# A graph attention kernel: attention scores stored word by word instead of turned on TensorE

## The reference

```
h = relu(layernorm(x))
x = x + adj @ norm((adj + adj.T) / 2 + I) @ h       # norm: by the row sums, both sides
h = relu(layernorm(x))
Wh    = h @ W                       # 8 heads of 64 columns
e_src = sum(Wh * a1), e_dst = sum(Wh * a2)          # one score per node and head, each
e     = leaky_relu(e_src[:, None] + e_dst[None, :], 0.2), -9e15 where adj == 0
out_h = elu(softmax(e) @ Wh)
x     = x + dense layers 512-256-128-256-512 (concatenated out_h)
```

## Time and profile before

| | us |
|---|---|
| median of 3 runs | 861.61 (861.1 to 862.35) |
| profiled execution | 862.1 |
| its span, first to last instruction | 860.3 |
| TensorE busy | 839.7 (98%) |
| VectorE busy | 700.0 (81%) |
| ScalarE busy | 428.7 (50%) |
| GpSimd busy | 281.0 (33%) |

### The profile page before, as it was taken

How to read it: one execution, slowest core, us unless ns; L and a number is a source line. 1 busy time by engine, 2 the same in 40 slices (tenths; PEclk the granted TensorE clock), 3 DMA queues, 4 the chain that set the end, 5 groups by cost and what they waited for, 6 DMA issues and landing times.

```text
span 860.3 us, 15286 instructions
## 1 busy us (share of the span) xinstructions
PE 839.7 (98%) x5208; PEld 756.5 (88%) x5208; DVE 700.0 (81%) x1222; ACT 428.7 (50%) x797; POOL 281.0 (33%) x299
## 2 busy tenths in 40 slices
PE   2999999999999999999999999999999999999997
PEld 2888888888888888888899999999999999999786
DVE  6899886557656886586999999999999999998864
ACT  3445433221111112257766666666666666775753
POOL 0000000000000000057875555555556654566422
PEclk9999999999999999999999999999999999999999
DMA  8979931703222222053310000000000032000134
GB/s 344 406 272 375 362 98 50 219 0 122 96 97 92 95 93 89 0 196 126 129 27 25 23 16 26 26 24 25 26 26 25 24 93 68 26 2 6 45 148 149
DMA packets 37675, 87.97 MB, mean 102 GB/s; under 512 B 7216, under 2 KB 8368, under 8 KB 37616
## 3 DMA queue, kind: packets, MB, share of 16 engines
q1 hardware_dynamic: 37616, 87.24, 28.5%
HBM read 74.45 MB, written 12.78 MB: 101 GB/s over the span
## 4 chain that ended last, share of the span: by engine, by line
PE 97%; DMA 1%; DVE 1%; ACT 1%; SPq 0%; issue 0%
PE bank L1877 29%; PE bank L1921 14%; PE bank L77 13%; PE bank L79 13%; PE bank L78 13%; PE bank L554 3%; PE bank L1082 2%; PE bank L1087 2%; PE bank L1083 2%; DMA l_kept<-adj 1%; PE bank L1033 1%; PE bank L2455 1%; PE bank L2449 1%; PE bank L2394 1%; PE bank L2451 1%; PE bank L2420 0%
## 5 line engine op out<-in xcount | busy, mean ns | idle before, releaser
L1397 DVE SCALAR_TENSOR_TENSOR l_q<-bank,e,mask 128x512 fp32r<-128x512 f32 x512 | 339.0, 740 | 22.9 <-PE bank L1877 22.9
L1877 PE MATMUL bank<-l_parts,l_q 128*128 128x260 f32 x2048 | 249.6, 283 | 0.0
L1877 PEld LDWEIGHTS bank<-l_parts,l_q 128*128 128x128 f32 x2048 | 246.7, 188 | 0.4
L77 PE MATMUL bank<-x_hi,s_hi 128*128 128x512 f32 x448 | 174.4, 389 | 0.0
L79 PE MATMUL bank<-x_hi,s_lo 128*128 128x512 f32 x448 | 174.3, 389 | 0.0
L78 PE MATMUL bank<-x_lo,s_hi 128*128 128x512 f32 x448 | 174.3, 389 | 0.0
L805 POOL TENSOR_TENSOR l_prod<-wh,l_a 128x512 f32<-128x512 f32 x29 | 34.0, 1195 | 379.5 <-ACT wh L757 379.5
L1565 ACT ACTIVATE l_o_q<-bank 128x260 f32<-128x260 f32 x128 | 49.0, 388 | 104.0 <-PE bank L1877 96.7
L79 PEld LDWEIGHTS bank<-x_hi,s_lo 128*128 128x128 f32 x448 | 84.1, 188 | 17.6
L78 PEld LDWEIGHTS bank<-x_lo,s_hi 128*128 128x128 f32 x448 | 84.1, 188 | 17.3
L77 PEld LDWEIGHTS bank<-x_hi,s_hi 128*128 128x128 f32 x448 | 84.1, 188 | 17.3
(11 more groups left out here) (234 smaller groups left out, 1179.8 us busy)
## 6 DMA issues: line engine op xcount, KB each, us to landing
rows<-adj_t SPq DMA_DIRECT2D x48, 512.0 KB, 3.8
l_now<-adj SPq DMA_DIRECT2D x16, 512.0 KB, 7.5
l_rows_k<-adj_t SPq DMA_DIRECT2D x16, 512.0 KB, 8.3
l_src<-e_rows SPq DMA_DIRECT2D x32, 256.0 KB, 3.2
l_kept<-adj SPq DMA_DIRECT2D x12, 512.0 KB, 13.2
wh_store<-wh SPq DMA_DIRECT2D x4, 1040.0 KB, 6.2
l_h<-x SPq DMA_DIRECT2D x4, 1024.0 KB, 17.3
x<-x SPq DMA_DIRECT2D x1, 4096.0 KB, 13.7
```

The lines of the kernel that those rows point to most:

```text
L77: pe.matmul(acc, hi, rhs_hi, start=first, stop=False, skip_group_check=True)
L1397: v.scalar_tensor_tensor(out=q[:, i, :], in0=bank[S_BANKS[hh]][:], scalar=e[:, i, H + h:H + h + 1], in1=mask[:, i, cols], op0=ALU.is_le, o ...
L1877: return pe.matmul(bank[Q_BANKS[hh][t]][:, 0:PW], q[:, i, t * P:(t + 1) * P], parts[pair_slot][:, i, hh * PW:(hh + 1) * PW], start=i == 0, ...
```

## The change

The turning of scores by TensorE goes, with the copies behind it. `e_rows` becomes an array of 16 tiles x 16 scores x 128 nodes, and SyncE stores straight out of `e`, where a partition holds one node: each run that is written is one word. The first group's first two columns go first, its other 14 columns by tile after `keep_wh(1)`, the other groups whole. `load_src` reads four runs of 128 scores for one of 512. `wa_hi` and `wa_lo` come to lie side by side, so that one product makes hi x hi and hi x lo (32 columns), and VectorE adds both halves when it takes them. A sixth tile is chosen ahead, at k = 13. Waits of ScalarE, GpSimd and TensorE on the turned scores go. The path for rows that overflow, which does not run here, is adapted alike.

```diff
-        e_t = rows[0:2 * H, 2, :]
...
-        wa_hi = sb("l2_wa_hi", [P, KC, 2 * H], F32R, side="right")
-        wa_lo = sb("l2_wa_lo", [P, KC, 2 * H], F32R, side="right")
+        wa_parts = sb("l2_wa_parts", [P, KC, 4 * H], F32R, side="right")
+        wa_hi, wa_lo = wa_parts[:, :, 0:2 * H], wa_parts[:, :, 2 * H:4 * H]
...
-        EARLY_Q = {11: 0, 12: 1, 14: 2, 15: 3, T: 4}
+        EARLY_Q = {11: 0, 12: 1, 13: 2, 14: 3, 15: 4, T: 5}
...
-            def store_e(q):
-                sp.wait_ge(e_copied, q + 1)
-                sp.dma_start(e_rows[:, q * 512:(q + 1) * 512], turned_e(q, e_late)).then_inc(stored if q >= 2 else first_stored, 16)
-            store_e(0)
-            sp.wait_ge(first_stored, 16)
+            def store_scores(tiles, cols, done):
+                count = cols.stop - cols.start
+                if count == 1:
+                    src, dst = e[:, tiles, cols.start], e_rows[tiles, cols.start, :].rearrange("t p -> p t")
+                else:
+                    src = e[:, tiles, cols].rearrange("p t c -> p (t c)")
+                    dst = e_rows[tiles, cols, :].rearrange("t c p -> p (t c)")
+                sp.dma_start(dst, src, allow_slow_non_contiguous=True).then_inc(done, 16)
+            sp.wait_ge(e_ready, 2 * SLOTS + 4)
+            for h in range(2):
+                store_scores(GROUPS[0], slice(h, h + 1), first_stored)
+            sp.wait_ge(first_stored, 32)
             spread_scores(0)
             keep_wh(0)
             keep_wh(1)
+            for t in range(SLOTS):
+                store_scores(slice(t, t + 1), slice(2, 2 * H), stored)
             keep_wh(2)
-            store_e(1)
-            sp.wait_ge(first_stored, 32)
+            sp.wait_ge(e_ready, 2 * 2 * SLOTS + 4)
+            store_scores(GROUPS[1], slice(0, 2 * H), first_stored)
+            sp.wait_ge(first_stored, 48)
             spread_scores(1)
             keep_wh(3)
-            store_e(2)
-            store_e(3)
-            sp.wait_ge(stored, 32)
+            for q in range(2, 4):
+                sp.wait_ge(e_ready, 2 * SLOTS * (q + 1) + 4)
+                store_scores(GROUPS[q], slice(0, 2 * H), stored)
+            sp.wait_ge(stored, 16 * (SLOTS + 2))
...
-                    v.tensor_copy(e[:, t, :], bank[7][:, 0:2 * H]).then_inc(e_ready, 2)
+                    v.tensor_reduce(e[:, t, :], bank[7][:, 0:4 * H].rearrange("p (k c) -> p c k", k=2), AX_X, ALU.add
+                                    ).then_inc(e_ready, 2)
...
-                if k in (8, 13):
-                    take_e_t((k - 8) // 5)
...
-                    mm = split_product(pe, bank[7][:, 0:2 * H], g_hi[:, b, cols], g_lo[:, b, cols],
-                                       wa_hi[:, k, :], wa_lo[:, k, :], k == 0)
+                    pe.matmul(bank[7][:, 0:4 * H], g_hi[:, b, cols], wa_parts[:, k, :], start=k == 0, stop=k == KC - 1,
+                              skip_group_check=True)
+                for k in range(KC):
+                    cols = slice(k * P, (k + 1) * P)
+                    mm = pe.matmul(bank[7][:, 0:2 * H], g_lo[:, b, cols], wa_hi[:, k, :], start=False, stop=k == KC - 1,
+                                   skip_group_check=True)
...
-                if k == 7:
-                    turn_e(range(0, 4))
-                if k == 11:
-                    turn_e(range(4, 8))
-            turn_e(range(8, 12))
...
-                        row = e_rows[r // 4 * 2 + hh:r // 4 * 2 + hh + 1, r % 4 * QW:(r % 4 + 1) * QW]
-                        sp.dma_start(src[:, hh, :], row.to_broadcast([P, QW])).then_inc(src_loaded[hh], 16)
+                        row = e_rows[r % 4 * GT:(r % 4 + 1) * GT, r // 4 * 2 + hh:r // 4 * 2 + hh + 1, :].rearrange("t o p -> o t p")
+                        sp.dma_start(src[:, hh, :].rearrange("p (t n) -> p t n", t=GT), row.to_broadcast([P, GT, P])).then_inc(src_loaded[hh], 16)
...
-                late_scores(a, 2, e_late[:])
...
-                        late_scores(a, 3, e_late[:])
...
-                        if hp == 0 and r == 0:
-                            a.wait_ge(stored, 32)
...
-                p.wait_ge(first_stored, 32)
...
-                        pe.wait_ge(e_copied, 4)
...
-                    q_phase(r, pair_slot, 0, lambda i: last_turns(pe) if isinstance(r, int) and r == 0 and i == G8 else None)
+                    q_phase(r, pair_slot, 0)
```

More of the change, by code:

```diff
@@ L653, in spread_and_project @@
         e_ready = sem("l2_e_ready")
-        e_turned = sem("l2_e_turned")
-        e_copied = sem("l2_e_copied")
         top_ready = sem("l2_top_ready")
@@ L673, in per_head, with sync @@
             return ap.rearrange("p (h d) -> p h d", h=H)
-        def turned_e(q, e_late=None):
-            return (e_t if q < 2 else e_late)[:, q % 2 * 512:(q % 2 + 1) * 512]
-        def sync(sp, spread_scores, keep_wh, e_late):
+        def sync(sp, spread_scores, keep_wh):
             first_sync(sp)
@@ L793, in late_factors @@
             a.activation(fac["D"][:], args[1][:], ACT.Exp, scale=-1.0).then_inc(fac_ready, 1)
[L794 to L797, removed]
         def gpsimd(p, between):
@@ L931, in vector @@
                     v.tensor_tensor(w_lo[:], w_rows, w_hi[:].bitcast(F32), ALU.subtract).then_inc(w_ready, 1)
-                    v.tensor_copy(wa_hi[:], wa[:]).then_inc(w_chain, 1)
+                    v.tensor_copy(wa_hi, wa[:]).then_inc(w_chain, 1)
                 if r == 1:
                     v.wait_ge(w_chain, 4 * KC + 2)
-                    v.tensor_tensor(wa_lo[:], wa[:], wa_hi[:].bitcast(F32), ALU.subtract).then_inc(w_ready, 1)
+                    v.tensor_tensor(wa_lo, wa[:], wa_hi.bitcast(F32), ALU.subtract).then_inc(w_ready, 1)
             norms(0)
@@ L960, in reduce_e @@
                     v.wait_ge(top_steps, 3)
-                    v.tensor_copy(e[:, t, :], bank[7][:, 0:2 * H]).then_inc(e_ready, 2)
+                    v.tensor_reduce(e[:, t, :], bank[7][:, 0:4 * H].rearrange("p (k c) -> p c k", k=2), AX_X, ALU.add
+                                    ).then_inc(e_ready, 2)
                     v.wait_ge(e_ready, 2 * t + 5)
-            def take_e_t(q):
-                v.wait_ge(e_turned, q + 1)
-                v.tensor_copy(turned_e(q), bank[4 + q % 2][0:2 * H, :]).then_inc(e_copied, 1)
             v.sem_inc(e_ready, 4)
@@ L1098, in tensor @@
             pe.wait_ge(w_ready, 2)
[L1099 to L1108, removed]
             def turn_more(t, b):
@@ L1111, in turn_more @@
                     turn(t, b)
-            for k in in_turns(T, (turn_more, 0), (project, 1)):
-                if k == 7:
-                    turn_e(range(0, 4))
-                if k == 11:
-                    turn_e(range(4, 8))
-            turn_e(range(8, 12))
[L1118 to L1127, removed]
+            for _ in in_turns(T, (turn_more, 0), (project, 1)):
+                pass
+        return ((sync, vector, scalar, gpsimd, tensor), (late_args, check_range, last_wh, factors, late_factors),
+                (wh_summed, wh_ready, e_ready), x1_stored, (first_stored, stored), fac_ready, len(EARLY_Q))
 def attend_and_finish(nc, before, bank, wh, e, mask, ident, adj, e_rows, fac, wh_store, x1_store, weights, weight_parts, small, out):
@@ L1320, in combine @@
             return first_head, second_head
-        (programs, (late_args, check_range, last_wh, factors, late_factors, late_scores, last_turns), (wh_summed, wh_ready, e_ready, e_copied),
+        (programs, (late_args, check_range, last_wh, factors, late_factors), (wh_summed, wh_ready, e_ready),
          x1_stored, (first_stored, stored), fac_ready, early_q) = before
@@ L1343, in keep_wh @@
                                  wh[:, tiles, :, :].rearrange("p t h e -> p t (h e)")).then_inc(wh_stored, 16)
-                sync_before(sp, load_src, keep_wh, e_late[:])
+                sync_before(sp, load_src, keep_wh)
                 for r in range(2, LAST + 1):
```

8 lines of the change are left out of this document (4 added, 4 removed).

## The result

The changed kernel takes 937.08 us (median of four) against 861.63 in the same rounds; the ratio is 1.0862, 95% interval 1.0842 to 1.0882. The forecast was 860.4, its range 859.0 to 877.

A forecast was written before the change was run, and what follows sets the result against it. TensorE, 97% of the span, was taken as the bound: 2.17 us leaves its stream, 1.2 is gained after the wait for `last_wh`, words hidden; profile 862.1 - 1.2 = 860.9, median 860.4. Range 859.0 to 877.

The forecast's parts named there:

- I take 15, the nearest: SyncE's word stores: each word costs an engine 15 ns, from the bias loads, with 9.3 as low end.
- high end of 27.9: SyncE's word stores: a word as dear as a 512-byte run, 27.9 ns per engine, giving 876.4 us.
- even at 28 ns they and `src` land by 392: First two score columns and the row load behind them: there by 392, ScalarE having waited until 398.14.
- first rival: Words too dear: from 19.1 ns `fill_src(2, 0)` is late and TensorE stands; 876.4 us at 27.9 ns; 36 in 100.
- Latest 452.9: ScalarE's filling for row 2: `src` may come as late as 452.9, so a word up to 19.1 ns.
- the forecast's sum: SyncE's queue: `src` of row 2 is there at 423.6 + 1.536w, 446.6 at 15 ns a word.
- in runs of 512 bytes: nothing: Later row loads, now 0.9 us by the line, are asked for a round of 23 us ahead and cost nothing.
- TensorE's part: Projection through first pass: 2.17 us leaves TensorE's stream, 1.2 gained, with a 1.0 us wait for `last_wh` after six products.
- VectorE moves by 0.41: VectorE's work from `cut_turned(14)` to the last scores comes 0.41 us earlier, not 1.74, and `last_wh` with it.
- The sixth tile costs 0.4 us of the gain: Chosen tile added at k = 13 on VectorE: without it VectorE and `last_wh` would move by 0.88 us.
- Two more inputs are nearly as late: VectorE's last chosen tile (427.27) and GpSimd's remainder half (427.85) come just before the first pass's end, 428.35.
- second rival: All of TensorE's work comes off, `last_wh` being in time: 2.17 us gained, 859.5 us; 15 in 100.

The follow-up runs named there:

- experiment 1: Stores alone, no kernel computed: several word and run patterns from one tile, each waited for; 512 words landed in 1.9 to 18.0 us by their addresses.
- experiment 7: The change with words 64 bytes apart in a scratch array, still waited for, loaded rows stored in 256-byte runs; 888.10 us, ratio 1.0299.
- experiment 2: The change without words: score groups stored in runs of 256 bytes, the first group whole, nodes in another order; 860.13 us, ratio 0.9979.
- experiment 11: On top of 10, `last_wh` moved ahead of ScalarE's wait for scores and the filling of bank 7; 860.23 us, ratio 0.9984.
- experiment 12: On top of experiment 11, `fill_src(0, 1)` moved behind the parts of the first head's last quarter; 859.19 us, ratio 0.9972.
- experiment 3: On top of experiment 2, five chosen tiles ahead instead of six; 860.47 us, ratio 0.9985.
- 9: The change with scores kept by column, groups stored in 16-byte runs, row loads of 2 KB, ScalarE ordering the nodes; 861.71 us, ratio 1.0002.
- 10: On top of 9, `fill_src(r + 1, 0)` moved behind the masks of tiles 8 to 15 in the next round; 860.30 us, ratio 0.9986.
- 8: The change with 64 unused bytes behind each row of 128, so tiles lie 9 KB apart; 913.14 us, ratio 1.0599.
- experiment 4: The change's words still issued, not waited for until the dense layers; loads wait only for added 256-byte run stores; 934.69 us, ratio 1.0824.

## Why the prediction was wrong

**The step that failed** is "I take 15, the nearest" in the words: a price per word and engine, read from the packets' share of DMA time. For the first store it was the wrong kind of price. The engines' time for the first two columns is (0.12 + 0.40) us x 16 / 1024, 8.1 ns a word, even under the low end of 9.3; but the landing, which the next load waits for, was 20.4 us for 64 words an engine. For whole groups it was the right kind and too low: by itself a group's packets took 41 ns a word and engine, above the high end of 27.9 (experiment 1). No bound from rows of reads could hold that, and the one write among them had runs of 520 words. The sentence "even at 28 ns they and `src` land by 392" fell first: `src` was there at 412.9.

**The range** had the first rival's sign, but not its place or size. Words too dear were to show at `fill_src(2, 0)` alone, with 16 us; they showed at three fillings, the first in the projection loop, since a store that lands late holds SyncE in its wait, the loads behind it, the stores of `wh`, and the next words. The rival also left out the clock, 8.1 us here. "Latest 452.9", the threshold of 19.1 ns, was worked out rightly for one queue of constant prices; with words 64 bytes apart, where that comes nearest, the third stand is indeed the one that stays (experiment 7). There a group took 17.06 us, 33 ns a word and engine with the landing, by which the forecast's sum has the row at 423.6 + 1.536 x 33 = 474; it landed at 481.5, 4.5 of the difference being the slower row load. For the change itself that sum, at 41 ns, would give 486.6; its row came at 530.8, behind two stands of TensorE (41 us) that the sum doesn't have.

**The row loads** "in runs of 512 bytes: nothing" was right for the runs and wrong here: 3.4 us at 9 KB between tiles, 7.7 at 8 KB. The array's shape cost it, not the length of the runs, and it cost time only behind late stores; in experiment 2 nothing waits for these loads.

**TensorE's part** held. Experiment 2 gained 1.7 (1.1 to 2.6 by its interval) for 1.2 forecast. The 2.17 came off the stream (TensorE's busy time falls from 839.7 to 837.4); `last_wh` left a gap of 0.75 after six products (forecast 1.0), as it did in the changed kernel itself:

```profile
438.18 2.05 PE L1852 MATMUL bank<-l_parts,l_q 128*128 128x260 f32 x15 [0.75 <-ACT wh L790]
```

"VectorE moves by 0.41" was short. Its loop of chosen tiles starts at 419.79 for 421.03, of which 0.43 is an earlier start of the whole stream in that execution (the first transposes of the second layer are at 363.98 for 364.41) and 0.8 the move. At `cut_turned(14)` it was still the forecast's (411.44 for 412.31, 0.44 without the earlier start); of the rest 0.3 is that VectorE's own last product took 0.99 us for 1.29. The forecast had no such term and no run shows its reason, so that part of the 1.7 was luck. "The sixth tile costs 0.4 us of the gain" has no support: five tiles were not faster. "Two more inputs are nearly as late" held for GpSimd: once the gap was gone, its remainder held the mask pass (experiment 11), and with both gone the second rival's 859.5 was reached (experiment 12: 859.2). VectorE's tiles, the other one, held the first pass in no run; with five ahead they held the third (experiment 3). The traces of 9 and 10 do name one of them as what ended the gap after six products, but `last_wh` ended there some 0.15 us before TensorE went on, as in experiment 2, and moving it took the gap away.

**A rule on patterns.** The Trainium skill, page "DMA: Bandwidth & Descriptors", section "Rules for kernel authors", would rearrange a pattern whose last dimension isn't contiguous. The traces agree: 8192 words land in 22.9 us as words, 1.4 in runs of 256 bytes. The 512 bytes that its "Specifications" want for line rate no run here tests, since 32 KB in 1.4 us are far from it; for the landing of so small a store, runs of 64 bytes (1.8 us) did nearly as well as 256.

**What stays open.** Which part of the memory path takes its time over words in the same 64 bytes, and over equal places 4 KB apart, no view shows; that such words are written one after another is the theory's picture, and what the runs show is that the time goes by the addresses. No run has the changes of experiments 7 and 8 together, so whether their 48 and 23 us of 76 add up is open.

## What to carry over

Price a small store by its landing, and by where its bytes go, not by packets or bytes: look at what waits for the landing, and at everything behind it on that queue. Where scores must cross from partitions to a row without TensorE, turn the layout so that each run has at least a few neighbouring words, and pay for the order where an engine has time. When a wait on one engine goes, look for the next input that is nearly as late before you count the gain.

## What was not expected of the hardware

- Single words to HBM: 512 land in 1.9 us if each has 64 bytes to itself, in 8.0 to 9.9 side by side, in 17.7 to 22.0 when the rows lie 8 KB apart, 8.3 to 9.8 at 9 KB. The DMA share is near zero most of that time (0.01 over the first 18.0 us of experiment 1), but not for 8192 words (0.92 over 22.9 us).
- Loads know it too: four runs of 512 bytes to all partitions take 7.7 us with the runs 8 KB apart, 3.4 at 9 KB.
- A transfer behind words on the same queue is held with them: 27 us for a load that takes 8 (experiment 4), and issues themselves stand for 15 to 29 us. On another engine's queue it took 9.7 for 3.1.
- ScalarE reads every fourth word of SBUF in 1.1 us where 512 in a row take 0.6.
